# Attention block in one kernel: two groups of values and maxima per slot instead of four, and a ring of six steps of probabilities

## What is computed

```python
qkv = einsum('bchw,oc->bohw', x, w_qkv)            # 3 x 512 rows
q, k, v = split(qkv); q, k, v: (b, 8 heads, 64, 1024); q *= 64**-0.5
attn = softmax(einsum('bhdi,bhdj->bhij', q, k))     # 1024 x 1024 per head
out  = einsum('bhij,bhdj->bhid', attn, v)           # back to (b, 512, 1024)
y = einsum('bchw,oc->bohw', out, w_out) + b_out
y = y * rsqrt(mean(y*y over channels) + 64**-0.5) * rms_scale
return y + x
```

## Time and profile before

| | |
|---|---|
| median of 3 runs | 4029.89 us (4027.57 to 4030.04) |
| the profiled execution | 4027.74 us, of which the span from first to last instruction is 4026.0 us |
| TensorE (PE) busy | 3951.3 us, 98% of the span |
| VectorE (DVE), ScalarE (ACT), GpSimd (POOL) busy | 2890.0, 2320.3, 2919.8 us |
| mean granted TensorE clock | 0.993 |

### The profile page before, as it was taken

One profiled execution on the slowest core, in us unless ns is written; L12 is line 12 of the kernel. 1 busy time (PEld: TensorE's weight loads), 2 busy tenths in 40 slices (PEclk: granted clock), 3 DMA queues, 4 the chain that ended last, 5 costly groups with the idle time before them and its releaser, 6 DMA issues.

```text
span 4026.0 us, 53767 instructions
## 1 busy us (share of the span) xinstructions
PE 3951.3 (98%) x18624; PEld 2427.4 (60%) x18624; DVE 2890.0 (72%) x3279; ACT 2320.3 (58%) x4044; POOL 2919.8 (73%) x2279
## 2 busy tenths in 40 slices
PE   7999999999999999999999999999999999999996
PEld 5666665666656666666666666666666565666652
DVE  5667777777767777677776777777677777777775
ACT  4556565565655656556565655656556565565653
POOL 4668676786776868767686776867768676786866
PEclk9999999999999999999999999999999999999997
DMA  3111111111111111112011020111111111111100
GB/s 148 42 44 51 53 51 59 49 53 43 64 53 42 54 41 69 48 42 74 32 64 53 35 71 32 63 53 37 69 53 43 53 57 55 46 53 42 66 19 32
DMA packets 71275, 212.22 MB, mean 53 GB/s; under 512 B 8152, under 2 KB 8280, under 8 KB 58208
## 3 DMA queue, kind: packets, MB, share of 16 engines
q1 hardware_dynamic: 71008, 208.80, 14.7%
HBM read 168.92 MB, written 39.85 MB: 52 GB/s over the span
## 4 chain that ended last, share of the span: by engine, by line
PE 94%; DVE 3%; issue 2%; POOL 1%; ACT 0%; DMA 0%; POOLq 0%; SPq 0%; ACTq 0%; DVEq 0%
PE pv L648 23%; PE aux L485 17%; PE score L626 14%; PE score L635 11%; PE aux L516 9%; PE aux L542 9%; PE aux L611 6%; PE pv L567 3%; PE aux L592 2%; DVE inv_sum L968 1%; DVE maxima L910 1%; DVE k_l L903 1%; DVE y_sb L981 0%; DVE aux L916 0%; ACT probs L715 0%
## 5 line engine op out<-in xcount | busy, mean ns | idle before, releaser
L1070 POOL TENSOR_TENSOR prob_sum<-prob_sum,probs 128x512 f32<-128x512 f32 x1536 | 1966.3, 1308 | 376.8 <-ACT probs L715 375.1
L715 ACT ACTIVATE probs<-score 128x512 f32<-128x512 f32 x2048 | 1109.4, 594 | 871.2 <-PE score L635 863.7
L916 DVE TENSOR_REDUCE aux<-aux 128x1 f32<-128x513 f32 x640 | 446.7, 698 | 849.7 <-PE aux L611 636.3
L648 PE MATMUL pv<-probs,v_sb 128*64 128x512 f32 x4096 | 993.3, 606 | 0.0
L626 PE MATMUL score<-q_hl,k_hh 128*128 128x512 f32 x2048 | 868.8, 424 | 5.8 <-ACT probs L715 5.8
L635 PE MATMUL score<-q_hm,k_l 72*128 72x512 f32 x2048 | 815.6, 398 | 0.7 <-DVE q_hm L928 0.7
L1066 POOL TENSOR_TENSOR prob_sum<-probs 128x512 f32<-128x512 f32 x256 | 338.3, 1343 | 505.9 <-ACT probs L715 505.9
L485 PE MATMUL aux<-x_hi,w_ring 128*128 128x512 f32 x2048 | 657.0, 398 | 12.0 <-POOL x_lo L309 11.2
L626 PEld LDWEIGHTS score<-q_hl,k_hh 128*128 128x128 f32 x2048 | 387.2, 189 | 267.5 <-issue 158.7
L648 PEld LDWEIGHTS pv<-probs,v_sb 128*64 128x64 f32 x4096 | 248.3, 136 | 482.4 <-issue 435.4
L910 DVE TENSOR_REDUCE maxima<-aux 128x1 fp32r<-128x1024 f32 x384 | 465.9, 1213 | 0.0
(11 more groups left out here) (84 smaller groups left out, 4984.8 us busy)
## 6 DMA issues: line engine op xcount, KB each, us to landing
w_ring<-w_split SPq DMA_DIRECT2D x93, 1024.0 KB, 4.8
x_stage<-x SPq DMA_DIRECT2D x128, 256.0 KB, 4.0
resid<-x SPq DMA_DIRECT2D x128, 256.0 KB, 4.1
out<-resid SPq DMA_DIRECT2D x128, 256.0 KB, 2.0
w_split<-w_ring SPq DMA_DIRECT2D x3, 1024.0 KB, 12.4
w_split<-y_sb SPq DMA_DIRECT2D x3, 1024.0 KB, 3.8
y_sb<-wqkv SPq DMA_DIRECT2D x4, 512.0 KB, 8.1
probs<-wqkv SPq DMA_DIRECT2D x2, 512.0 KB, 6.9
```

The costliest lines, as they stand in the source:

```text
L648: pe.matmul(pv[half][e * D:(e + 1) * D, :], v_sb[:, pair // 2, j, (pair % 2) * P + e * D:(pair % 2) * P + (e + 1) * D], probs[:, j % 4, e, ...
L715: act.activation(probs[:, j % 4, e, :], score[e][:], ACT.Exp, scale=SOFT).then_inc(prob_ready, 1)
L916: dve.tensor_reduce(aux[:, first:first + 1], aux[:, k * HALF:first + 1], AX_X, ALU.max).then_inc(aux_free[k], 1)
L1070: pool.tensor_tensor(prob_sum[:, e, :], prob_sum[:, e, :], probs[:, j % 4, e, :], ALU.add).then_inc(prob_added, 1)
```

## The change

- The four groups of a slot become two. Place 1: values of steps 4 and 5 of the slot before, maxima of tile 0, values of steps 6 and 7, sums, maxima of tile 1. Place 9: values of steps 0 and 1, tile 2, values of steps 2 and 3, tile 3.
- Values now run up to six steps behind the scores, so `probs` holds 6 steps instead of 4. The room comes from the residual's buffer: x pieces and residuals share one `stage` of four.
- Items: the first at 3, the second in two halves at 5 and 7 (for slot 6: V1 at 3, K0 whole at 5, K1 whole at 7 instead of 15), O0 at 11, O1 at 13, Q with T at 15 as before.
- Maxima: only head 0 of tiles 1 and 3 is reduced in two parts, all others at once.
- Tables are set anew; pieces 4 and 6 of x go to VectorE at (6,4) and (6,5), the others to GpSimd.

```diff
-INVERT_SUMS_AT = ((2, 5), (2, 5), (2, 6), (2, 2), (2, 5), (2, 5), (2, 2), (2, 2))
-NORMALISE_AT = (6, 6, 6, 4, 6, 6, 4, 4)
-OUTPUT_HIGH_AT = (7, 7, 7, 6, 7, 7, 6, 6)
-REPEAT_Q_AT = (0, 3, 3, 0, 0, 2, 0, 0)
+PLACES = 2 * STEPS
+RING = 6
+INVERT_SUMS_AT = ((2, 2),) * 8
+NORMALISE_AT = (2,) * 8
+OUTPUT_HIGH_AT = (4, 8, 4, 4, 4, 4, 4, 4)
+REPEAT_K_AT = (8, 9)
-SPLIT_SECOND = (2,)
+SPLIT_MAXIMA = (1, 3)
-MEAN_AT = ((0, 7), (1, 7))
-INVERT_AT = (((0, 11), (0, 15)), ((1, 11), (1, 15)))
+MEAN_AT = ((0, 3), (1, 7))
+INVERT_AT = (((0, 4), (0, 8)), ((1, 8), (1, 14)))
-SCALE_AT = ({1: (1, 2), 2: (1, 3), 3: (1, 6)}, {2: (2, 5), 3: (2, 10)})
+SCALE_AT = ({1: (1, 1), 2: (1, 3), 3: (1, 4)}, {2: (2, 4), 3: (2, 5)})
-SPLIT_HIGH_AT = ((5, 0), (5, 0), (5, 2), (5, 2), (6, 2), (6, 4), (6, 6), (6, 10))
-SPLIT_LOW_AT = ((5, 0), (5, 0), (5, 2), (5, 2), (6, 5), (6, 6), (6, 9), (6, 12))
-SPLIT_BY = ((0, 1, 4, 6), (2, 3, 5, 7))
+SPLIT_HIGH_AT = ((5, 0),) * 4 + ((6, 0),) * 4
+SPLIT_LOW_AT = ((5, 0), (5, 0), (5, 0), (5, 0), (6, 4), (6, 0), (6, 5), (6, 0))
+SPLIT_BY = ((4, 6), (0, 1, 2, 3, 5, 7))
...
+    if t == 5 and slot == 6 and projected:
+        out.append(("K0", 1))
+    if t == 7:
...
+        elif slot == 6 and projected:
+            out.append(("K1", 2))
...
+def in_halves(slot, name):
+    return name == {0: "K1", 1: "V1", 2: "K1", 3: "V3", 4: "K1", 5: "V0", 7: "V3"}.get(slot)
...
@@ TensorE, one(body) @@
-                            for j in (2 * g - 2, 2 * g - 1):
-                                if g > 0:
-                                    values(body, slot, j, False)
...
-                            if f"M{g}0" in names:
-                                maxima_of_tile(body, slot, g)
+                        elif t == 1:
+                            if preceding:
+                                values(before[0], before[1], 4, before[2])
+                                values(before[0], before[1], 5, before[2])
+                            if "M00" in names:
+                                maxima_of_tile(body, slot, 0)
+                            if preceding:
+                                values(before[0], before[1], 6, before[2])
+                                values(before[0], before[1], 7, before[2])
                                 sums(body, slot)
+                            if "M10" in names:
+                                maxima_of_tile(body, slot, 1)
+                        elif t == 9:
+                            values(body, slot, 0, False)
+                            values(body, slot, 1, False)
+                            if "M20" in names:
+                                maxima_of_tile(body, slot, 2)
+                            values(body, slot, 2, False)
+                            values(body, slot, 3, False)
+                            if "M30" in names:
+                                maxima_of_tile(body, slot, 3)
@@ ScalarE, exponentials @@
-                        act.wait_ge(pv_done, n - 7)
...
+                    step = (body.b * SLOTS + slot) * STEPS + j
+                    if step >= RING:
+                        act.wait_ge(pv_done, 2 * (step - RING) + e + 1)
+                        act.wait_ge(prob_added, adds_until(step - RING, e))
+                    act.activation(probs[:, step % RING, e, :], score[e][:], ACT.Exp, scale=SOFT
@@ VectorE, item @@
-                    if name[2] == "1" and int(name[1]) not in SPLIT_SECOND:
+                    if name[2] == "1" or int(name[1]) not in SPLIT_MAXIMA:
```

More of the change, by code:

```diff
@@ L396, in store_half @@
                     sp.wait_ge(resid_added, 4 * (2 * b + half) + m + 1)
-                    sp.dma_start(out_v[b, m, :, half * HALF:(half + 1) * HALF], resid[:, m, :]
+                    sp.dma_start(out_v[b, m, :, half * HALF:(half + 1) * HALF], stage[:, m, :]
                                  ).then_inc(out_stored[m], 16)
-            def wait_stored(halves):
-                for m in range(MT):
-                    sp.wait_ge(out_stored[m], 16 * halves)
             def one(body):
@@ L441, in _ @@
                 store_half(B - 1, half)
-            wait_stored(2 * B)
+            for m in range(MT):
+                sp.wait_ge(out_stored[m], 16 * 2 * B)
         @block.tensor
@@ L474, in wait_x, with project @@
             def wait_x(body, half):
[L476 to L481, removed]
+                n = body.b + 1
+                for by in SPLIT_BY if n else SPLIT_FIRST:
+                    pieces = [c for c in by if c < KT * (half + 1)]
+                    if pieces:
+                        wait_piece(pe, pieces[-1], n)
+            def project(out_ap, w, cols, xcols, turn=None, ks=range(KT)):
+                for k in ks:
                     for n, (wp, xp) in enumerate(((0, x_hi), (1, x_hi), (0, x_lo))):
@@ L487, in project, with item @@
                 return last
-            def item(body, slot, name, turn=None):
+            def item(body, slot, name, turn=None, part=None):
                 if name == "Q":
@@ L519, in item @@
                                 n += 1
-                    last.then_inc(aux_full[k], 1)
+                    if part != 0:
+                        last.then_inc(aux_full[k], 1)
                 elif name == "T":
@@ L657, in one @@
                         pe.wait_ge(k_repeated, 4)
+                    before = (body, SLOTS - 1, True) if slot == 0 else (body, slot - 1, False)
+                    preceding = not (body.first and slot == 0)
                     for t in range(PLACES):
-                        g = t // 4
                         names = [name for name, _ in items_at(slot, t, body.first, body.last)]
@@ L679, in one @@
                                     item(body, slot, name)
-                        else:
-                            for name in names:
-                                item(body, slot, name)
             pe.wait_ge(const_loaded, 64)
@@ L694, in _ @@
             last = Body(epi, B - 1, False, True)
-            for j in (STEPS - 2, STEPS - 1):
+            for j in range(STEPS // 2, STEPS):
                 values(end, SLOTS - 1, j, True)
@@ L819, in split_x @@
                 act.activation(x_hi[:, c % KT, (c // KT) * HALF:(c // KT + 1) * HALF],
-                               x_stage[:, c % XS, :], ACT.Copy).then_inc(xhi_ready, 1)
+                               stage[:, c % XS, :], ACT.Copy).then_inc(xhi_ready, 1)
             def one(body):
                 for slot in range(SLOTS):
+                    preceding = not (body.first and slot == 0)
                     for t in range(PLACES):
@@ L869, in _ @@
             act.wait_ge(spill_set, 1)
+            act.wait_ge(mask_set, 2)
             run_bodies(act, one)
             end = Body(epi, B, False, True)
+            for m in (2, 3):
+                square(end, 0, m)
             copy_sums(B * SLOTS, 0)
@@ L1009, in one @@
                                     scale_y(body, half, m)
-                        if t == OUTPUT_HIGH_AT[slot] and slot not in LOW_BY_GPSIMD:
-                            split_output_low(dve, body.b * SLOTS + slot)
                         if (slot, t) in SPLIT_LOW_AT and not body.last:
@@ L1022, in _ @@
             split_w(0, 0)
[L1023 removed]
+            for c in SPLIT_FIRST[0]:
                 split_x(dve, c, 0)
@@ L1106, in one @@
                     for j in range(STEPS):
-                        if j == OUTPUT_LOW_AT and slot in LOW_BY_GPSIMD and not (body.first and slot == 0):
+                        if j == OUTPUT_LOW_AT and not (body.first and slot == 0):
                             split_output_low(pool, body.b * SLOTS + slot)
```

216 lines of the change are left out of this document (110 added, 106 removed).

## The result

The changed kernel takes 4146.23 us (median of 4 runs, 4139.04 to 4147.45) against 4029.93, a ratio of 1.0287 with a 95% interval of 1.0273 to 1.0302. The forecast was 4088, the range 4050 to 4125. The direction was right and the size was half of what came. The profiled execution has a span of 4144.0 us, 118.0 more than before, and a mean granted clock of 0.983.

The account below looks back on a forecast made before the run. TensorE's own stream, busy 98% of the span, was taken as the bound. On 4027.7 us, - 51 - 10 + 29 + 16 + 26 + 32 + 7 gave 4077, and 11 for the clock gave 4088 us, range 4050 to 4125.

Parts of the forecast that it names:

- 1  fewer switches: Every slot: scores left and entered twice instead of four times, 0.40 us a slot over 127 slots, gain 51 us.
- 2  slot 2's old wait: Slot 2: no maxima pass stands two places behind K0 any longer, so its wait goes, gain 10 us.
- 3  tile 3: Place 9 group: tile 3 waits for VectorE's reductions of tile 2, 0.23 us over 127 slots, loss 29 us.
- 4  slot 0: Slot 0: VectorE's list makes its reduction of tile 2 1.05 us late, so tile 3 waits, 15 batches, loss 16 us.
- 5  slot 5: Slot 5: ScalarE's high output part waits for normalise and delays step 3's exponential; TensorE loses 1.7 us a batch, 26 us.
- 6  slot 6, the wait: Slot 6: K1 at place 7 waits for piece 6, split after K0's low part, 2.1 us in 15 batches, loss 32 us.
- 8  clock: Loop: new idle stretches of 1.7 and 2.1 us lower TensorE's clock one time in four, loss 11 us, bounds 0 and 45.
- ends: Last batch's slots 5 and 6 lose 2.3 us each to ScalarE's block, the first slot 2.5 us, loss 7 us.
- The unseen one: Switch from maxima directly to values, absent from the old trace: priced at 0.10 + 0.03 us.
- 0.76 for the piece: Slot 6: VectorE's time to split piece 6 of x, counted within the wait of K1.

Follow-up runs that it names:

- e1: Changed kernel with only piece 6 of x moved from (6,5) to (6,4), ahead of K0's low part: 4083.77 us, ratio 1.0134.
- e2: Changed kernel with only ScalarE's high part of the output in slot 5 moved from place 4 to 8: 5 to 9 us below the expected 4123 us.
- e4: Changed kernel with only slot 0's second half of the mean-square inversion moved from place 8 to 10: 5 to 9 us below the expected 4131 us.
- s1: The kernel of e5 with head 0 of all tiles again reduced in two parts: 4038.04 us, ratio 1.0018.
- c2: Changed kernel with GpSimd's adds of steps 2 and 3 in slot 2 cut to 8 of 512 columns: 4107.13 us.
- e3: Changed kernel with only slot 2's scaling of y's last quarter moved from place 5 to 10: 5 to 9 us below the expected 4126 us.
- c1: Changed kernel with GpSimd's adds of steps 2 and 3 in slot 6 cut to 8 of 512 columns: 4147.74 us.
- b2: The kernel of e5 with tile 2 first in slots 3, 5, 7, slot 2's scalings both at 10, output's high part at 8 in slots 6, 7: 3990.56 us.
- e5: Changed kernel with four moves: piece 6 to (6,4), slot 5's high part to 8, slot 2's last scaling and slot 0's second inversion to 10: 4009.8 us.
- e6: Changed kernel with the moves in slots 0, 2 and 5 only, slot 6 left as the change has it: 4078.21 us, ratio 1.0122.

## Why the prediction was wrong

In its own terms, forecast against what the trace and the slot lengths give (worked out as said in the last column):

```
part                        forecast   came    from
1  fewer switches             - 51     - 49    two exits of scores, two first scores: 0.39 x 127
2  slot 2's old wait          - 10     - 10    gone
-  slot 2's new wait             0     + 22    22.1 in PE's waits
3  tile 3                     + 29     + 23    0.42 + 0.42 against 0.34 + 0.32 at its pairs: 0.18 x 127
4  slot 0                     + 16     + 16    slot 0: 0.88 + 0.39 - 0.18 = 1.1, x 15
5  slot 5                     + 26     + 24    slot 5: 1.36 + 0.21 = 1.6, x 15
6  slot 6, the wait           + 32     + 45    2.93 and a weight load 0.1, x 15
8  clock                      + 11     + 28    slot 6: 4.80 + 0.21 - 3.03 = 2.0, x 14
-  ends                       +  7     + 17    5.0 + 10.1 + 1.0 + 1.0
-  left over                     0     +  2    slot 1 is 0.3 longer than the change alone gives, x 14, and rounding
sum                           + 60     + 118
```

**Right:** the switches (part 1). The unseen one, maxima to values, costs at its exit what maxima to scores did, 0.10 above the 0.22 of a pair; timeline of the changed kernel:

```profile
1293.13 0.39 PE L613 MATMUL aux<-k_hh,q_hm 64*128 64x512 f32 x1
...
1293.45 1.94 PE L669 MATMUL pv<-probs,v_sb 128*64 128x512 f32 x8
...
1295.22 1.03 PE L588 MATMUL pv<-prob_sum,ones_d 128*64 128x512 f32 x4
```

0.32 and 1.77 us, as in the earlier trace rows. The Trainium skill ("TensorEngine Tiling (Array Packing)", Key Properties) has every change of the tiling mode drain the engine; the trace agrees so far as this switch is not free. Right too: the mechanisms and places of parts 3 to 6, and with them the sign; e1, e2, e4 and s1 confirm each. Part 3 came out a fifth smaller.

**Wrong, first: part 6's term for the piece, and slot 2, which had no term.** "0.76 for the piece" is a mean over 64 pieces. In the traced loop half of them ran with GpSimd idle and none took over 0.93. At its new place piece 6 meets an add that has just begun, and takes 1.60: 45 us instead of 32. The same view of the kernel before had the warning, a tensor_tensor of the same shape, both inputs in SBUF, beside GpSimd's adds:

```profile
L321 DVE TENSOR_TENSOR o_lo<-o_norm,o_hi 128x512 fp32r<-128x512 f32 x16 | 28.3, 1770 | 0.0
```

Part 2 called slot 2's 10.0 us "free" and put nothing in their place. It looked at K0 alone and never added up VectorE's list for tile 2, where the change moves the second scaling from place 10 to 5, ahead of K1's low part. The new wait is 22 us. At 1.26 us a scaling, their mean in the kernel before, it would have been some 0.6 us a batch instead of 1.5 (an estimate from the 3.39 us they took); at the 0.71 of c2 it is gone, and with one of the two moved away too (e3). c1 and c2 show that GpSimd's adds make the durations. Together 35 us.

**Wrong, second: the clock.** "I take one in four" was a guess between bounds. The trace of before had one case, 1.40 us and a second pause, and that lowered it. In the batches 0 to 14 the changed kernel had 14 falls, all behind slot 6's 15 waits. For 2.0 us (c1) it is about every second time; the 1.3 to 1.5 us in slots 5 and 2 never did it there. So the 0.9 us of the first error may have made the second larger. That length alone does not decide is shown by slot 1, where in e1 and c1 the clock fell once each behind two waits of some 0.5 and 0.6 us. The Trainium skill ("TensorE: Matmul & The Clock Gate", Why this matters for your kernels) warns only of longer gaps; that did not hold here, and the measurement decides.

**Wrong, third, smaller: the ends.** ScalarE's block in the last batch's slots 5 and 6 costs 10.1 us, not 4.6. TensorE waits 3.7 us in each, where I had set 2.3 against the kernel before, and the clock falls there both times, which I had not counted. Moving the block to place 8 takes 6.4 us out of slot 5 (e2) and 5.6 out of slot 6 (b2). Of the 2.5 us that I had for the first slot at most 1.2 came, but the time before the first scores grew by 5.0, which I had not counted. Its cause stays open: the kernels that share this prologue have their first scores at 55.2 to 59.0 us in the traces, the kernel before at 54.0 and s1 at 52.8, so head 0's late bank is a part of it, by one trace.

## What to carry to other kernels

When a full engine's stream is shortened, list for each work item that moved what stands before it in its own engine's list, and compare the end of that with the new time at which it is wanted; a gain of 0.4 us a slot was lost to four items that missed by 1 to 3 us, and a place one earlier or two to five later in a table cured each. Do it for every slot, also where an old wait goes. Take a VectorE duration at the place where the instruction will run: with two SBUF inputs beside a busy GpSimd it was over twice what it was alone (1.60 against 0.69, 1.7 against 0.71). A single idle stretch of 2 us on TensorE can cost nearly as much again through its clock (1.6 us in c1).

## What the runs showed of the hardware

- A scaling on VectorE that lasts 0.75 us alone lasted 7.84 us beside seven GpSimd instructions without a gap. That is more than waiting for the one that had begun, and it came and went from batch to batch in the same program: in 4 batches of e5, 3 of c1, one each of e1 and e2, and in no other trace.
- When a scaling and a GpSimd instruction started within 0.1 us of each other, either could be the slow one (1.91 and 1.31 us, or 0.75 and 1.84), and this differed between batches of one run.
- The same wait of 2.9 us lowered TensorE's clock in 14 of 15 batches in one kernel (e6) and in 8 of 15 in another (c2). What decides it stays open.
